# Conv attention on TensorE: queries and row sums between the two pairs of shifted scores, values and projections behind them, with two holds on GpSimd

## The reference, cut to what matters

```python
q = einsum('bchw,oc->bohw', gn(x), qW).reshape(B, 8, 1024, 32)   # 8 heads, 1024 queries of 32
k = conv1x1(bn(depthwise3x3_stride2(gn(x))), kW)                 # 256 keys of 32, one set for all heads
v = the same with its own weights                                # 256 values of 32
attn = softmax(q @ k / 2)                                        # 8*1024 rows of 256
ctx = attn @ v
x = x + einsum('bchw,oc->bohw', ctx, oW)
```

## Time and profile before

| | us |
|---|---|
| median of 3 runs | 2136.09 |
| lowest and highest run | 2134.69 and 2139.86 |
| the profiled execution: its time | 2136.72 |
| the profiled execution: its span | 2135.0 |
| conv attention in it, first pair of shifted scores to last | 53 to 796 |
| an image in its middle | 46.8 |

### The profile page before, as it was taken

One profiled execution on the slowest core, in us unless ns is written; L12 is line 12 of the kernel. 1 busy time (PEld: TensorE's weight loads), 2 busy tenths in 40 slices (PEclk: granted clock), 3 DMA queues, 4 the chain that ended last, 5 costly groups with the idle time before them and its releaser, 6 DMA issues. The chain is left out here.

```text
span 2135.0 us, 45465 instructions
## 1 busy us (share of the span) xinstructions
PE 1921.1 (90%) x11956; PEld 1401.0 (66%) x11956; DVE 1415.9 (66%) x3732; ACT 987.3 (46%) x2210; POOL 1364.3 (64%) x1623
## 2 busy tenths in 40 slices
PE   3999999999999998889888988886199999999997
PEld 2555555555555544656655665664199999999997
DVE  3777787877777756787887778876444444444443
ACT  0555555555555553544443444332055555555554
POOL 1666666667666652455545554554578888888887
PEclk8999999999999999999999999998599999999999
DMA  5333232323232212111111111111245445444454
GB/s 200 79 71 75 64 76 63 72 63 76 61 76 69 69 32 90 47 38 40 39 42 35 40 37 42 36 41 47 62 59 66 64 64 66 62 66 64 64 66 50
DMA packets 175444, 132.08 MB, mean 62 GB/s; under 512 B 33437, under 2 KB 164933, under 8 KB 175301
## 3 DMA queue, kind: packets, MB, share of 16 engines
q0 software_dynamic: 55808, 52.50, 15.4%
q1 hardware_dynamic: 118341, 77.16, 13.9%
q10 hardware_dynamic: 1152, 0.54, 0.1%
HBM read 31.47 MB, written 46.71 MB: 37 GB/s over the span
## 5 line engine op out<-in xcount | busy, mean ns | idle before, releaser
L1769 POOL DMA_INDIRECT out<-f_y,f_rows x272 | 423.8, 1558 | 45.7 <-POOL f_waited L1767 40.2
L492 DVE TENSOR_REDUCE neg_max<-s_bank 128x2 f32<-128x512 f32 x512 | 329.0, 683 | 79.1 <-PE s_bank L784 77.1
L1832 DVE SCALAR_TENSOR_TENSOR f_hidden<-f_silu,f_rows,f_h_bank 128x341 f32<-128x341 f32 x272 | 155.4, 571 | 305.5 <-ACT f_silu L1801 280.7
L1201 POOL DMA_INDIRECT routed<-a_rows,a_target_idx x256 | 251.7, 983 | 68.8 <-issue 68.8
L619 ACT ACTIVATE probsT<-st_bank 128x512 f32<-128x512 f32 x512 | 277.7, 596 | 11.3 <-PE st_bank L802 11.0
L1578 PE MATMUL a_score_bank<-t_eT,t_gT 128*128 128x512 f32 x512 | 247.9, 608 | 1.2 <-DVE a_val L1245 1.2
L375 POOL TENSOR_TENSOR odd_sums<-probsT 128x512 f32<-128x512 f32 x128 | 176.2, 1396 | 108.0 <-ACT probsT L619 107.7
L1880 PE MATMUL f_y_bank<-w,f_hiddenT 114*128 (+1 forms) x1632 | 230.3, 277 | 1.3 <-ACT f_hiddenT L1793 1.3
L802 PE MATMUL st_bank<-q_stack,k_stack 98*128 98x512 f32 x512 | 219.0, 473 | 3.8 <-ACT probsT L619 2.0
L1211 POOL TENSOR_TENSOR a_causal_probs<-a_causal_probs,a_tril 128x128 f32<-128x128 f32 x128 | 58.3, 456 | 248.7 <-DVE a_causal_probs L1297 241.6
L1880 PEld LDWEIGHTS f_y_bank<-w,f_hiddenT 114*128 114x128 f32 (+1 forms) x1632 | 203.1, 191 | 8.3 <-issue 1.8
(11 more groups left out here) (224 smaller groups left out, 3815.9 us busy)
## 6 DMA issues: line engine op xcount, KB each, us to landing
q_stack<-q_high SPq DMA_DIRECT2D x512, 64.0 KB, 2.2
f_rows<-routed SPq DMA_DIRECT2D x272, 66.0 KB
q_stack<-q_low POOLq DMA_DIRECT2D x256, 64.0 KB, 2.4
out<-X SPq DMA_DIRECT2D x16, 512.0 KB, 3.2
X<-in_x SPq DMA_DIRECT2D x1, 6144.0 KB, 21.7
out<-f_y,f_rows POOLq DMA_INDIRECT x272
q_stack<-max_rows SPq DMA_DIRECT2D x256, 4.0 KB
routed<-a_rows,a_target_idx POOLq DMA_INDIRECT x256
```

The lines of the kernel that those rows point to most:

```text
L492: dve.tensor_reduce(neg_max[:, i % 2, CT * j:CT * (j + 1)], s_bank[h % 2][:], AX_X, ALU.max, negate=True).then_inc(max_ready, 1)
L1201: pool.indirect_dma_start(out=routed, out_offset=bass.IndirectOffsetOnAxis(ap=target_idx[:, slot, t, k:k + 1], axis=0), in_=rows[:, slot, ...
L1769: pool.indirect_dma_start(out=out, out_offset=bass.IndirectOffsetOnAxis(ap=rows[:, i, TOKEN:TOKEN + 1].bitcast(I32), axis=0), in_=y[:, i, ...
```

## The change

Five things are done in the order of the calls. On TensorE `queries` and `row_sums` move from behind scores 2 and 3 to between `turn_maxes` and the second pair of shifted scores; `group_variances` and `group_means` move ahead of scores 0 and 1. On ScalarE `query_high` moves ahead of the second two exponentials. On VectorE `query_low` moves ahead of row maxima 2 and 3, `group_variance` to the head of unit 0, and the first `add_output` from the middle of unit 6 to the end of unit 5. On GpSimd the adds of units 3 and 5 now also wait for VectorE's `scale` of that unit, and those of unit 7 for `spread`. No instruction that computes is added or removed.

```diff
 # GpSimd, add_keys(b, i)
                     if i % 2 == 0:
                         wait(pool, sums_full, octet_no(b, i // 2) - 1)
+                    if i in (3, 5) and has(b - 1):
+                        pool.wait_ge(scaled, 2 * (b - 1) + (1, 2)[i == 5])
+                    if i == PAIRS - 1 and has(b + 2):
+                        pool.wait_ge(spread_ready, b + 3)
 # VectorE, period
                         scored = pair(b, slot, i + LEAD)
+                        if i == 0 and has(new):
+                            group_variance(new)
...
-                        if i == 6 and has(b - 1):
-                            add_output(b - 1, 0)
-                        if i == 0 and has(new):
-                            group_variance(new)
                         if i == PAIRS - 1 and has(b + 2):
                             group_spread(b + 2)
+                        if i in Q_AT:
+                            ahead, k = Q_AT[i]
+                            if has(b + ahead):
+                                query_low(b + ahead, k)
                         if has(scored[0]):
                             row_max(scored[0], scored[2], 2)
                             row_max(scored[0], scored[2], 3)
...
+                        if i == 5 and has(b - 1):
+                            add_output(b - 1, 0)
 # ScalarE, period
-                        if has(b):
-                            exps(b, i, 1)
                         if i in Q_AT:
                             ahead, k = Q_AT[i]
                             if has(b + ahead):
                                 query_high(b + ahead, k)
+                        if has(b):
+                            exps(b, i, 1)
 # TensorE, period
                             shifted_scores(b, slot, i, 0)
+                        if i == 0 and has(new):
+                            group_variances(new)
+                        if i == PAIRS - 1 and has(b + 2):
+                            group_means(b + 2)
...
                             turn_maxes(*turning)
+                        if i in Q_AT:
+                            ahead, k = Q_AT[i]
+                            if has(b + ahead):
+                                queries(b + ahead, k)
+                        if i % 2 and has(summed[0]):
+                            row_sums(summed[0], summed[2])
                         if has(b):
                             shifted_scores(b, slot, i, 1)
...
```

More of the change, by code:

```diff
@@ L570, in period @@
                             split_keys(new, nslot)
-                        if i in Q_AT:
-                            ahead, k = Q_AT[i]
-                            if has(b + ahead):
-                                query_low(b + ahead, k)
                         if i == 0 and has(new):
@@ L867, in period @@
                             turn_maxes(*turning)
+                        if i in Q_AT:
[4 more added lines that the diff above has]
+                            row_sums(summed[0], summed[2])
                         if has(b):
                             shifted_scores(b, slot, i, 1)
-                        if i == 0 and has(new):
-                            group_variances(new)
-                        if i == PAIRS - 1 and has(b + 2):
-                            group_means(b + 2)
                         if has(scored[0]):
@@ L878, in period @@
                             keys_values(new)
-                        if i in Q_AT:
-                            ahead, k = Q_AT[i]
-                            if has(b + ahead):
-                                queries(b + ahead, k)
                         if i % 2 == 0 and has(summed[0]):
                             values(*summed)
-                        if i % 2 and has(summed[0]):
-                            row_sums(summed[0], summed[2])
                         if i == 5 and has(b - 1):
```

## The result

The change takes 2075.55 us (median of 4 runs, 2068.77 to 2077.44) against 2135.97 (4 runs of before): a ratio of 0.9705, 95% interval 0.9685 to 0.9724, so 2.95% faster by the ratio of the runs; the medians are 60 us apart, 2.8%. The forecast was 2063 within 2046 to 2098.

A forecast was written before the change was run, and what follows sets the result against it. TensorE was taken as the bound, waiting 6.2 us of each 46.8 us image. Gains of 64 us over 14 images, 6 for images 0 and 15, and 3 for image 7 made 73: 2063 us, range 2046 to 2098.

The forecast's parts named there:

- The bound: Conv attention: TensorE, though drawn busy, waits 6.2 us of a 46.8 us image, 3.8 of it on ScalarE's exponentials.
- Queries and row sums between, -3.8: Second pair of shifted scores: the moved work fills a 0.47 us stall in all eight units, 3.8 us an image.
- The cover gone in unit 3: Unit 3 shortens, but unit 4's scores wait 1.07 us for VectorE's maxima; the two units gain 0.76 us together, not 2.
- GpSimd's holds: Scaling of unit 5 falls from 3.05 to 1.2 us, dmean from 2.03 to about 0.2; TensorE's score waits behind them go.
- `add_output`: First residual add at unit 5's end: queries of unit 6 no longer wait about 0.5 us for it.
- The sum for an image, 42.2: Floor 40.6 us plus 1.2 of remaining waits plus 0.4 for new neighbours: 42.2 us, a gain of 4.6 an image.
- the floor: TensorE's work in an image without waits, summed from timeline distances: 40.6 us, with four score matmuls at 0.47.
- The new neighbours: Work newly adjacent on TensorE, such as transpose to queries: from nothing to 1.6 us an image, taken as 0.4.
- The edges and the kernel: Images 0 and 15 gain 3 us each, image 7's disturbance 3 once; with 64 from 14 images, 73 us.
- VectorE's order: Rival 0.14: maxima behind `q_low` in even units come late, taking half the gain back; kernel at 2098 us.
- GpSimd did not become the bound: Rival 0.04, slower: GpSimd's held adds lag beyond 4 us of slack; with 10 us of lag the kernel takes 2156.
- the stall moved only where it was said: Rival 0.05: next pair or scores wait as long instead, image stays 46.8 us; the prediction itself expected moving in unit 3.

The follow-up runs named there:

- sums_behind: The change with the row sums put back behind scores 2 and 3: 2108.87 us against 2147.55 for the kernel before, ratio 0.9809.
- holds_only: The kernel before with only GpSimd's three added waits and no order changed: 2148.27 us against 2151.46, ratio 0.9985.
- The early statistics: The change with the first half of the channel statistics moved from unit 2 to unit 1 on VectorE: 2081.36 us against 2155.11 before, ratio 0.9669.
- order_only: The change without GpSimd's added waits: 2092.6 us against 2151.46 for the kernel before, ratio 0.9728.

## Why the prediction was right, and where its terms were off

*The bound.* Right: TensorE waited in its second pair for ScalarE's exponentials. The two runs with the row sums, one each way, and the rows of the change show it for odd units; the units of sums_behind beside those of holds_only show it for even ones.

*Queries and row sums between, -3.8.* The waits on exponentials are gone from all eight units. What each unit gained differs: 0.39 in unit 1, 0.68, 0.97 and 0.47 in 5, 6 and 7.

*The cover gone in unit 3.* Right to 0.1: unit 3 was put at 3.6 us and is 3.70, the wait in unit 4 was put at 1.07 and is 1.06, and the two units together gain 0.72 where 0.76 was put. The early statistics show that it is VectorE's chain.

*GpSimd's holds.* The durations were right (1.20 and 0.16), and GpSimd's lateness cost nothing. What failed is the sentence "TensorE's share of that is what its scores waited for behind them": that share is zero in an ordinary image of the kernel before and 0.20 us an image in the new order. The 2.4 us of waits outside the exponentials lay mostly elsewhere, namely in maxima ahead of the scaling (0.56 in unit 3, 0.3 in unit 5) and in unit 6, where queries stand behind the residual add (0.48). In unit 3 of image 8 of before:

```profile
448.48 1.27 DVE L492 TENSOR_REDUCE neg_max<-s_bank 128x2 f32<-128x512 f32 x2
449.81 0.30 PEld L784 LDWEIGHTS s_bank<-k_stack,q_stack 96*128 96x128 f32 x2 [0.30 <-DVE neg_max L492]
450.24 0.62 PE L825 MATMUL sum_bank<-t_eT,ones_at 128*32 128x512 f32 x2
```

Scores 2 and 3 take 1.03 there (449.21 in the earlier trace rows to 450.24) and wait for maxima that are through at 449.75, while the scaling starts only at 449.87. I had read a wait of TensorE beside a long VectorE instruction as caused by it, without checking which maximum the score asks for. The waits went all the same, and all but 0.20 of them without the holds (order_only): the order took them, so that this part of the sum came out by luck.

*`add_output`.* Put at 0.5 us gained. It is more: without this edit the queries' move alone makes the kernel slower (unit 6 takes 1.53 more there), and taking it back costs 2.3 us an image on average, 1.9 without the images in which the clock fell.

*The sum for an image, 42.2.* Mis-sized by 0.75, or 10 us in 14 images. `group_variances` costs 0.25 instead of nothing or at most 0.1: pair and statistics take 0.94 in unit 0 where 0.69 was counted, and its weight load waits for the second residual add (4.2 us in the 11 images from 200 to 700 us). Scores 0 and 1 of units 0, 2, 3, 6 and 7 take 0.53 to 0.61 where the floor had 0.47 (before, they took as long, but for unit 7 with 0.48): 0.5 an image. The new neighbours come to some 0.3, within the 0.4 allowed: row sums start 0.20 behind the transpose instead of 0.11, scores ahead of values take 0.1 more, and queries with pair 0.1 to 0.2 less.

*The edges and the kernel.* Image 0 takes 5.0 us less than before where 3 were put, and with the other edges some 4 of the 10 us come back: conv attention ends 66.9 us earlier in the profiled execution, where 73 were put, and that execution takes 2068.8 against 2063.7. The other 7.5 us of the 12.5 between forecast and result have no mechanism behind them: the forecast took 0.7 off for the profiled execution of before standing above its median, and that of the change stands 6.8 below its own.

*The rivals.* VectorE's order took nothing back that could be measured, GpSimd did not become the bound, and the stall moved only where it was said.

## What to carry to other kernels

When an engine alternates between two banks with another one, put work that depends on neither between the two rounds, and then look at once for what that work itself needs: here a residual add in the wrong place, and a scaling that fell behind GpSimd, turned the gain into a loss. A lock-out of an engine is worth only what somebody waits for behind it, so name the instruction that a wait asks for before you price the lock. After such a move, walk the unit with the least work of its own: it tells which chain is next, and shortening that one was worth another 0.55 us an image.

## What the runs showed of the hardware

VectorE's instructions that read two SBUF tensors wait for a GpSimd add in flight, however small they are: dmean, one element in each partition, takes 0.16, 1.07 or 2.03 us, and up to 2.29 in the run with the queries alone. A cast with one SBUF input waits too: 32x256 takes 0.28 alone and 0.97 to 1.05 behind an add. How long depends on whether GpSimd's next add is already due. In the run with the row sums alone the second add comes 0.7 us after the first has ended, and the scaling gets in between:

```profile
448.29 1.29 POOL L375 TENSOR_TENSOR t_gT<-probsT 128x512 f32<-128x512 f32 x1
...
448.86 1.81 DVE L514 TENSOR_TENSOR context<-raw,rsum 128x1024 f32<-128x1024 f32 x1
450.29 1.51 POOL L375 TENSOR_TENSOR t_gT<-probsT 128x512 f32<-128x512 f32 x1 [0.71 <-ACT probsT L619]
```

That is the rule that the prediction cited from the Trainium skill ("SBUF — State Buffer", "Who interferes with whom"), and the trace agrees: 0.7 of waiting and 1.1 to 1.2 of work. Where the second add is due before the first ends, VectorE waits for both, 3.05 us in the earlier trace rows. One instruction at a time is thus too kind an estimate for a queue that is full. Near a tie the recorded starts do not tell who goes first: in unit 3 of image 8 of before the second add is recorded from 449.81 and lasts 2.39 us, while the scaling, recorded from 449.87, takes its 1.20; in image 7 the scaling is recorded from 399.66, 0.04 ahead of the first add, and takes 3.65.

A second pair that waits costs more than its wait: the matmul behind a held one starts 0.34 us after it, behind a free one 0.23 (distances between starts in the kernel before, in its second and its first pairs). Why is not shown.

TensorE's granted clock can fall behind a wait of 1.8 us, and need not: with the residual add back in unit 6 it did so in four of the 14 images that have this wait, at 1.6 us each.
